# One block for the four phases, TensorE outside the joins, next phase's products, constants and rows early, and the directed phase's results two units later

## What is computed

```python
h = jnp.maximum(_layernorm(x, axis=-1), 0.0)
x = x + _L0_gnn_ref(h, adj, ...)   # attention, 12 heads, adj added to the scores, output projection Wo
x = x + _L1_gnn_ref(h, adj, ...)   # twice: scores h @ (h Wleft)^T and h @ (h Wright)^T under the graph, then relu(norm)
x = x + _L2_gnn_ref(h, adj, ...)   # twice: softmax(h h^T), then three linear maps for lower, own and upper neighbours
x = x + _L3_gnn_ref(h, adj, ...)   # attention, 12 heads, masked by adj, no output projection
...
hl = h @ wl.T + b_l
hs = h @ ws.T + b_s
hr = h @ wr.T + b_r
ctx = jnp.einsum('bij,bjd->bid', attn * upper, hl) + diag_a[..., None] * hs + jnp.einsum('bij,bjd->bid', attn * lower, hr)
o = (ctx - mean) / jnp.sqrt(var + LN_EPS) * g + beta
```

## Time and profile before

| | |
|---|---|
| median of 3 runs | 2728.71 us (2727.24 to 2729.51) |
| profiled execution | 2728.7 us |
| its span in the trace | 2727.0 us |
| mean granted clock of PE | 0.992 |
| PE busy | 2657.1 us (97%) |
| DVE, ACT, POOL busy | 1793.2, 1247.8, 1088.2 us (66, 46, 40%) |
| DMA | 183.87 MB, 67 GB/s over the span |

### The profile page before, as it was taken

How to read it: one execution, slowest core, us unless ns; L and a number is a source line. 1 busy time by engine, 2 the same in 40 slices (tenths; PEclk the granted TensorE clock), 3 DMA queues, 4 the chain that set the end, 5 groups by cost and what they waited for, 6 DMA issues and landing times. The chain is left out here.

```text
span 2727.0 us, 78262 instructions
## 1 busy us (share of the span) xinstructions
PE 2657.1 (97%) x31118; PEld 2315.9 (85%) x31118; DVE 1793.2 (66%) x4041; ACT 1247.8 (46%) x2184; POOL 1088.2 (40%) x1075
## 2 busy tenths in 40 slices
PE   6999999998999999999989999999999989999998
PEld 5888888887888888888878888888888878898897
DVE  6777777774555555555477777877877875666664
ACT  4444444454454444445443333433433435565564
POOL 2343434443322332332233435344434444455455
PEclk9999999999999999999999999999999999999999
DMA  4222222224112212211221111111111112222221
GB/s 143 75 68 62 59 67 73 73 73 146 37 54 82 82 36 59 82 36 55 74 76 51 57 45 52 56 40 56 58 40 51 61 53 74 88 86 82 89 85 62
DMA packets 187135, 183.87 MB, mean 67 GB/s; under 512 B 79616, under 2 KB 186880, under 8 KB 187008
## 3 DMA queue, kind: packets, MB, share of 16 engines
q1 hardware_dynamic: 187008, 181.99, 21.8%
HBM read 131.61 MB, written 50.33 MB: 67 GB/s over the span
## 5 line engine op out<-in xcount | busy, mean ns | idle before, releaser
L58 PE MATMUL banks<-w_hi,hT_hi 128*128 128x384 f32 x1152 | 402.0, 349 | 8.0 <-PEq L2517 7.0
L58 PE MATMUL banks<-hT_hi,w_hi 128*128 128x512 f32 (+1 forms) x954 | 367.7, 385 | 23.5 <-DVE l_qT L582 13.0
L58 PE MATMUL banks<-w_hi,hT_lo 128*128 128x384 f32 x1152 | 387.9, 337 | 0.0
L58 PE MATMUL banks<-w_lo,hT_hi 128*128 128x384 f32 x1152 | 387.4, 336 | 0.0
L58 PE MATMUL banks<-hT_hi,w_lo 128*128 128x512 f32 (+1 forms) x954 | 356.6, 374 | 0.0
L58 PE MATMUL banks<-hT_lo,w_hi 128*128 128x512 f32 (+1 forms) x954 | 355.6, 373 | 0.0
L1294 ACT ACTIVATE l_m<-banks 128x512 f32<-128x512 f32 x192 | 114.8, 598 | 397.5 <-PE banks L58 393.6
L305 POOL TENSOR_TENSOR l_s_d<-l_s_b,l_mx 128x768 f32<-128x768 f32 x128 | 188.7, 1474 | 222.4 <-DVE l_mx L607 207.2
L58 PE MATMUL banks<-w_hi,l_hT_hi 128*128 128x384 f32 x768 | 267.6, 348 | 5.1 <-DVE l_left L2137 3.5
L58 PE MATMUL banks<-w_hi,l_hT_lo 128*128 128x384 f32 x768 | 257.6, 335 | 0.0
L58 PE MATMUL banks<-w_lo,l_hT_hi 128*128 128x384 f32 x768 | 257.1, 335 | 0.0
(11 more groups left out here) (208 smaller groups left out, 6131.8 us busy)
## 6 DMA issues: line engine op xcount, KB each, us to landing
after_l<-l_xr SPq DMA_DIRECT2D x192, 192.0 KB, 1.9
l_xl<-after_l SPq DMA_DIRECT2D x37, 768.0 KB, 4.7
l_xr<-after_l SPq DMA_DIRECT2D x32, 768.0 KB, 4.5
xa<-in_x SPq DMA_DIRECT2D x16, 768.0 KB, 5.4
l_xr<-in_x SPq DMA_DIRECT2D x64, 192.0 KB, 2.4
l_xr<-after_l SPq DMA_DIRECT2D x64, 192.0 KB, 2.4
out_x<-l_xr SPq DMA_DIRECT2D x64, 192.0 KB, 1.9
xa<-after_l SPq DMA_DIRECT2D x11, 768.0 KB, 7.0
```

The source lines that it names most:

```text
L58: last = nc.tensor.matmul(out, lhs[a](c), rhs[b](c), start=(m == 0), stop=(m == n - 1))
```

## The change

All phases share one block, so that the barriers are gone. Each of DVE, ACT and POOL adds 1 to a new semaphore `ended` when its part of a phase is over; DVE, ACT, POOL and SP wait for all three before they touch the next phase (a multiple of 3), since tiles of one phase lie where those of the last lay. PE does not wait for it: it goes on into the next phase behind waits for single results (`shared["l2_ended"]` and the like hold a semaphore and its last count).

The first products of the next phase get banks of their own: four instead of two at the end of l0, two of them earlier in the last turn; six (left, right and own product of two tiles) at the end of l1; six queries and keys and two values at the end of l2. Constants, `adj` and, where their buffer is free, rows of the next phase are loaded in the phase before. The `handed_over` memsets move from DVE to POOL, before the last turn. The last results of l0, l1 and l3 are made on DVE (`own_result`, `centred`, `scaled`) where POOL made them or two engines passed them to and fro. The opening loads the first rows in two halves and each of Wq and Wk on its own semaphore, takes statistics a pair of tiles at a time, and makes products as soon as a weight is split. In the directed phase the results of a layer-1 unit (`finishes`) are added to `x` in the next layer-1 unit, two units later, and not in the layer-0 unit between; the first turn is written out ahead of the loop.

```diff
-    block = ctx.enter_context(nc.Block())
...
-            sp.dma_start(xl[:], rows(x_in, 0)).then_inc(xl_in, 16)
-            load_weights(sp, raw, own_weights, shared["w_loaded"])
-        n_consts = 0
-        for dst, src in biases(bv, out_bias, b_q, b_k, beta):
-            sp.dma_start(dst, src).then_inc(consts, 16)
...
+            first = rows(x_in, 0)
+            sp.dma_start(xl[:, 0:2, :], first[:, 0:2, :]).then_inc(xl_first, 16)
+            sp.dma_start(xl[:, 2:TILES, :], first[:, 2:TILES, :]).then_inc(xl_in, 16)
+            for s, signal in enumerate((wq_in, wk_in, shared["w_loaded"], shared["w_loaded"])):
+                sp.dma_start(raw[:, s], own_weights[s].rearrange("(c p) n -> p c n", p=P)).then_inc(signal, 16)
...
+            sp.wait_ge(shared["ended"], 3 * 3)
+            sp.wait_ge(stored, stored_before)
...
+            hT_parts(0, 0)
+            hT_parts(0, 1)
+            weights((0,))
+            hT_parts(0, 2)
+            hT_parts(0, 3)
+            weights((1,))
             statistics(1)
             shifts(1)
...
+        def product_of_next(j):
+
+            s, c = j // KC, j % KC
+            pe.wait_ge(w_lo_set, n_w + s + 1)
+            weight = tuple((lambda k, w=w: w[:, slot_of(s), k, c * P:(c + 1) * P]) for w in (w_hi, w_lo))
+            split_matmul(nc, banks[:, (1, 0, 2, 3)[j], :], weight, h_cols(slice(0, COLS))).then_inc(shared["m_done"], 1)
...
+            else:
+                pe.wait_ge(y_read, i * TILES - 1)
+                product_of_next(0)
...
             else:
-                pe.wait_ge(w_lo_set, n_w + 1)
                 pe.wait_ge(y_read, i * TILES)
-                product_of_next(0)
+                product_of_next(1)
             pe.wait_ge(eT_set, i * TILES + 3)
             exp_transposes(i, 3)
             if ahead:
                 pe.wait_ge(v_set, n * TILES + 1)
                 keys(n, 0)
             else:
-                product_of_next(1)
+                pe.wait_ge(eT_set, i * TILES + TILES)
+                out_transposes(i, 0)
             wait_apart(o_set, i * 2 + 1)
...
+                product_of_next(2)
+                product_of_next(3)
...
+            ended = shared["l2_ended"]
+            h_all = h_cols(slice(0, COLS))
+
+            def first_product(bank, s, c, signal):
+                split_matmul(nc, banks[:, bank, :], w_cols(s, slice(c * P, (c + 1) * P)), h_all).then_inc(signal, 1)
+
+            def first_values(t):
+                split_matmul(nc, banks[:, 6 + t, 0:D], h_cols(slice(t * P, (t + 1) * P)), w_cols(V, slice(0, D)))\
+                    .then_inc(v_done, 1)
+
+            pe.wait_ge(*ended["hT_set"])
+            pe.wait_ge(*ended["left_set"])
+            pe.wait_ge(*ended["w_lo_set"])
+            first_product(0, Q, 0, q_done)
+            pe.wait_ge(*ended["right_read"])
+            first_product(1, K, 0, k_done)
+            pe.wait_ge(*ended["s_set"])
+            first_product(2, Q, 1, q_done)
+            pe.wait_ge(*ended["self_set"])
+            first_product(3, K, 1, k_done)
+            first_product(4, Q, 2, q_done)
+            pe.wait_ge(*ended["hT_hi_set"])
+            first_product(5, K, 2, k_done)
+            pe.wait_ge(*ended["c_set"])
+            first_values(0)
+            first_values(1)
             pe.wait_ge(zeroed, 2)
-            wait_apart(k_set, 3)
+            pe.wait_ge(q_set, KC)
+            pe.wait_ge(v_set, 2)
+            wait_apart(k_set, KC)
             scores(0, 0)
             scores(0, 1)
-            values(0, 1)
             turns(pe, plain_turn)
 
...
+        sp.wait_ge(stored[1], stored_before[1])
+        load_rows(0, 1)
+        for k, name in enumerate(("L2_gnn_bl", "L2_gnn_br", "L2_gnn_bs")):
+            sp.dma_start(shared["l2_biases"][:, k], a[name][0].partition_broadcast(P)).then_inc(shared["l2_b_in"], 16)
...
+        centred(0)
+        centred(1)
+        last_scale(0)
+        centred(2)
...
+        step.catch_up(step.n - 3)
+        own_result(0)
+        step.catch_up(step.n - 2)
+        own_result(1)
+        step.catch_up(step.n - 1)
+        own_result(2)
+        step.catch_up(step.n)
+        own_result(3)
+        nc.vector.memset(shared["ends"][:, 2:3], 0.0).then_inc(shared["ended"], 1)
...
+            before = Unit(u.n - 2, u.q - 1, 1, 0) if finishes(u) else below if is_last(u) else None
...
-            left_copy(u, 1)
-            if ends:
-                result(below, 0)
-                result(below, 1)
+                left_copy(u, 1)
...
-            self_copy(u, 0)
+            if before is not None:
+                result(before, 0)
+                result(before, 1)
+            if below is not None:
...
             passed(0)
-            self_copy(u, 1)
-            if ends:
-                result(below, 2)
-                result(below, 3)
+            if below is not None:
+                self_copy(u, 1)
+            if before is not None:
+                result(before, 2)
+                result(before, 3)
...
+        dve.wait_ge(shared["ended"], 2 * 3)
+        dve.wait_ge(*shared["l1_ended"]["stored"])
...
+                right_part(u, 2)
+                passed(above, 1)
+                wait_apart(self_set, 2)
+                delta_transposes(u)
+                left_part(u, 3)
+                context(u, 0)
+            else:
                 left_part(u, 0)
...
+        ended, first = shared["l1_ended"], Unit(0, 0, 0, 0)
+
+        def first_product(bank, t, s, signal):
+            split_matmul(nc, banks[:, bank, 0:D], h_cols(first, t), projection(first, s)).then_inc(signal, 1)
+
+        pe.wait_ge(*ended["hT_set"])
+        pe.wait_ge(*ended["u_read"])
+        products(first)
+        pe.wait_ge(*ended["w_lo_set"])
+        pe.wait_ge(*ended["lin_set"])
+        first_product(0, 0, LEFT, left_done)
+        first_product(1, 0, RIGHT, right_done)
+        first_product(3, 1, LEFT, left_done)
+        pe.wait_ge(*ended["rows_set"])
+        first_product(4, 1, RIGHT, right_done)
+        pe.wait_ge(*ended["h_set"])
+        transposes(KC, rows_of[0], 0)
+        first_product(6, 0, SELF, self_done)
+        first_product(7, 1, SELF, self_done)
         schedule(unit, loop)
...
+        block = shared["block"] = ctx.enter_context(nc.Block())
```

More of the change, by code:

```diff
@@ L344, in projected_turn @@
             residual(i, 3)
-            result(i, 0)
-            if not ahead:
-                for t in (1, 2, 3):
-                    result(i, t)
+            if ahead:
+                result(i, 0)
         def plain_turn(i, opening, ahead, further):
@@ L1233, in ending @@
             root(i, k, 1)
-            if k >= 2:
-                for x in range(PAIR if isinstance(i, int) and i == last and k == 3 else TILES):
+            if k >= 2 and not (isinstance(i, int) and i == last and k == 3):
+                for x in range(TILES):
                     affine(i, k, x)
@@ L1317, in unit @@
             m_part(i, k, 1)
-            if not tail:
-                weight(CARRIED)
             ended(0)
@@ L1322, in unit @@
             m_part(i, k, 2)
-            if not tail:
-                weight(CARRIED + 1)
             ended(2)
@@ L1327, in unit @@
             m_part(i, k, 3)
+            if not tail:
+                weight(CARRIED)
             m_part(i, k, 4)
+            if not tail:
+                weight(CARRIED + 1)
             m_part(i, k, 5)
@@ L1354, in _ @@
         turn(last, False)
-        for x in range(TILES):
-            norm_rows(last, 3, x)
+        nc.scalar.activation(shared["ends"][:, 1:2], ident[:, 0:1], ACT.Copy).then_inc(shared["ended"], 1)
     @block.vector
@@ L1493, in unit @@
             passed(1)
+            if not tail:
+                dve.wait_ge(consts, 80)
+                dve.wait_ge(zeroed, 8)
             lin_copy(i, k, 0)
@@ L1792, in directed_phase, with finishes @@
     last = turns - 1
-    block = ctx.enter_context(nc.Block())
+    block = shared["block"]
     def pair_of_units(j):
         return Unit(2 * j + 2, j, 1, 0), Unit(2 * j + 3, j + 2, 0, 1)
+    def finishes(u):
+        return u.layer == 1 and not is_last(u) and not (isinstance(u.q, int) and u.q == 0)
     def is_last(u):
@@ L2030, in unit @@
                 next_weight(1)
+            if below is None:
+                weights((CARRIED, CARRIED + 1))
             passed(1)
@@ L2047, in loop @@
         def loop(turn):
-            with act.Fori(0, last) as j:
+            with act.Fori(1, last) as j:
                 turn(j)
         schedule(unit, loop)
+        nc.scalar.activation(shared["ends"][:, 1:2], ident[:, 0:1], ACT.Copy).then_inc(shared["ended"], 1)
     @block.vector
@@ L2199, in unit @@
         def unit(u, below, above, stats):
-            ends = below is not None and below.layer == 1
             carries = is_last(above)
+            before = Unit(u.n - 2, u.q - 1, 1, 0) if finishes(u) else below if is_last(u) else None
             def passed(c):
```

514 lines of the change are left out of this document (298 added, 216 removed).

## The result

The changed kernel takes 2692.95 us (median of 4 executions, 2689.87 to 2695.12) against 2728.4 of the kernel before, a ratio of 0.9868 with a 95% interval of 0.9856 to 0.988: 35 us faster. That is 16 us short of the 51.7 forecast, and 2.95 us above the range. The profiled execution was the fastest of the four, 2689.9 us with a span of 2688.1; it lies 38.8 us under the profiled one of before. Run again beside later experiments, the same kernel gave 2690.79 (2690.14 to 2692.88), ratio 0.9868, 0.9853 to 0.9884.

The account below looks back on a forecast made before the run. PE, busy 97%, was taken as the bound, leaving its idle, half-clock and stretched time to win. Terms 6.4 + 6.9 + 12.3 + 12.6 + 13.2 + 0.9 = 52.3 off 2728.7 gave 2676.4, forecast 2677; range 2667 to 2690.

Parts of the forecast that it names:

- Opening: Start of the kernel: separate weight semaphores, earlier loads and statistics, and later normalise shorten PE's waits; 6.4 us won.
- Join l0 to l1: End of l0: two more products cover 5.25 us idle and half-clock time returns; 6.9 us, bounds 3 and 7.
- Join l1 to l2: End of l1: six products replace the barrier stall and the slow stretch goes; 12.3 us, bounds 5 and 12.6.
- Rival B: At the joins PE stops for DVE or ACT, so they give half; +12 us, 2689, chance 0.15.
- Directed phase: l2's loop: 0.91 us won in each of 14 layer-0 units; 12.6 us, bounds 0 and 12.6.
- C: Directed loop gains nothing, its left copy being late for statistics and contexts too; +12.6 us, 2689, chance 0.12.
- E: Slower: four results in the layer-1 unit push its left copies late; 2741 at 4.6 us excess, chance 0.03.
- Join l2 to l3: End of l2: eight products cover 13.02 us idle and the half-clock loss returns; 13.2 us, bounds 8 and 15.7.
- rival F: No change: `ended` holds the engines as the barrier did and PE soon waits for them; 2728, chance 0.04.
- Tail: End of the kernel: POOL's last two additions of 1.94 us become DVE's at 0.52 each; 0.9 us won.
- The memsets: Before each join: ten POOL instructions ahead of the last turn, lying beside POOL's idle 60%; costed at nothing.
- Rival D: Code fetch shows on PE at each of three joins; 2683 at 2 us each, 2690 at 4.5, chance 0.04.

Follow-up runs that it names:

- its three causes mended: Changed kernel with tiles at the old kernel's places, carried-weight splits at the first directed unit's end, l2 constants loaded behind the next rows: 2678.51 us, ratio 0.9823.

## Why the forecast was wrong, step by step

- *Opening*, 6.4: measured 6.3, and the first product 5.0 earlier for 4.5. The second wait (1.88) went. That the sum agrees to 0.1 is luck, as the lead there differs by 4 us between traces with this opening. No run takes the parts of the opening one by one; they rest on the rows.
- *Join l0 to l1*, 6.9: 4.5. The mechanism was right, the products cover the end. The term was too large by PE's wait ahead of the last output's transposes, now 3.10 us and 1.89 before, and by the rows of l1's second group, which come late behind the constants of l2. For the results I had asked what their later stores and loads run into ("each has 50 us, nothing is near"), and not for these seven loads: the loads moved ahead have no term in the sum, though they stand in front of a load that DVE waits for. Moving them back took the gap away.
- *Join l1 to l2*, 12.3: 6.0, and this is the step that failed: "I leave 0.3 for a remaining wait". The bounds, 5 to 12.6, held it. A remaining wait of 4.56 us (1.04 and 3.52) stands there, and a stretch at half clock behind it that costs another 1.7: together the 6.3 us that are missing. The change moves `weights((CARRIED, CARRIED + 1))` to between `left_copy(u, 2)` and `left_copy(u, 3)`; I counted PE's six products and did not follow DVE's order in the first unit. With the splits behind the copies the join won 10.9. Rival B came true in size at this join alone, by another mechanism than `ended`.
- *Directed phase*, 12.6: 13.6 (14 times the 0.91 of the forecast is 12.7, not 12.6). Undoing the part alone took all of the loop's gain back. Rivals C and E are out.
- *Join l2 to l3*, 13.2: 14.1, with 0.36 us before the exponential's transposes. Holding PE showed 11 of it to be PE's going on; rival F is out. Of the other 3 us, the early loads and DVE's order were not taken apart.
- *Tail*, 0.9: −1.0. DVE's two additions take 1.03 us as forecast, but a stretch at half clock now lies over the last weighing but one (2.63 us for 1.60, below) and the transposes behind it, and costs some 1.7. It is not the change's: of the twelve traces with this tail four have this stretch and won −1.0 to −2.0 us, the eight others 0.3 to 1.8, 0.9 in the mean.

```profile
2712.60 1.60 PE L813 MATMUL banks<-l_vX,l_eT 64*64 64x33 f32 x96 [1.21 <-ACT l_eT L423]
```

```profile
2672.94 2.63 PE L890 MATMUL banks<-l_vX,l_eT 64*64 64x33 f32 x96 [1.21 <-ACT l_eT L459]
```

```profile
2684.76 1.03 DVE L711 TENSOR_TENSOR xr<-l_o_rows,xr 128x384 f32<-128x384 f32 x2
```

- *What the sum lacked*: 4.5 us in the l1 loop from where tiles lie, shown by the shifted kernel before (it lost 4.0) and by the three kernels with the old places (they lost nothing). The change moves buffers and tiny tiles in front of l1's; I looked for the cost of loads and instructions alone. The forecast sum with what each place differed by: 52.3 − 0.1 (opening) − 0.1 (l0) − 2.4 − 4.5 − 6.3 + 1.0 (directed loop) + 0.9 (last join) − 1.9 (tail) = 38.9, and the profile has 38.8.
- *The memsets*, put at nothing: they cost nothing that the trace shows, but not for the reason given. They don't stand before the last turn of the phase before; POOL runs them (nine or eight) behind the wait for `ended`, at 624.00, 1398.0 and 2217.0, and no engine waited for them.

Rival D needs a gap that the sequencer ends at a phase's first product. There is none: PE's idle time in the third join's window is 2.64 us, and it is made up of 1.59 and 0.69 before scores and 0.36 before transposes, all behind the first eight products. The row with 1.59 names no releaser, but PE's code waits there for the value copies, and ACT ended the last of them at 2225.64, 0.2 us before PE went on:

```profile
2224.30 1.34 ACT L454 ACTIVATE l_vX<-banks 64x192 f32<-64x192 f32 x4 [0.22 <-PE banks L58]
```

The page "Runtime: NRT & Kernel Launch" of the Trainium skill, section "Instruction fetch mechanics", says that a taken branch out of the window of two pages stalls. The branch at L824 shows no stall here; whether its target lay outside that window no run shows.

Two of the signs of being wrong came true beside the range: a slow stretch was left at the first and the second join, and each join kept more idle time than the 2 us named (5.1, 4.7 and 2.6).

With its three causes mended the change gives 2678.5 us, near the 2677 forecast; the mechanisms of the sum were there, and the forecast missed what the change did beside them. That the two numbers are so close is in part luck, as the sum's terms for the opening and the tail move by some us between executions.

## What to carry to other kernels

Line up two traces by the k-th matmul of the same kind and look at the lead from place to place: it finds losses that busy shares hide, such as a loop at 233 ns a matmul instead of 228. When a change adds tiles, buffers or small ones, look where the large ones come to lie, and keep it as it was until it is measured. And where a change lets one engine run ahead, read the other engines' new order up to the first thing it will wait for: splits of weights, or loads for the phase after next, cost what they stand in front of.

## What the runs showed of the hardware

- TensorE's pace depends on where in SBUF what it reads lies. Matmuls of 512 columns on l1's second h start 228 ns apart with that tile at byte 142976 or 149120, and on average 233 with it at 143008, 148704 or 148736 (the last is a multiple of 256); in the same loop those on the first h, whose tile did not move, kept their pace to 0.5 ns. In l2, with moving weights and a stationary h, it was 173 ns at 145216 and 175 at 145248. All tiles of a phase moved together, so which distance between which tiles decides was not found out. The Trainium skill's page "SBUF — State Buffer", section "Who interferes with whom", says that only the port pair shared by VectorE and GpSimd brings contention and that TensorE never waits on anyone; the kernel before and its shifted copy differ in no engine's work, so if the rule holds the loss is TensorE's own.
- Whether and when the clock falls behind the same stall differs between executions. The same kernel's opening was at 0.50 from 41.5 in one and from 44.0 in another, and the lead after it differed by 1.4 us. Behind the same wait of 3.52 us at the second join the clock fell in the changed kernel (0.51 above), and it stayed up in the kernel with `ends` padded, where that join won 7.6 us and not 6.0:

```profile
1416.20:1419.70 3.50, 3.50 (x63) 2.31 (x64) 2.54 (x4) 0.83 (x1) 0.00 (x0) 1.00 0.00 0
```

  Such stretches, and one wait for rows that was 0.58 us in one execution and 3.08 in another, are as large as what single edits win. PE stands less in the changed kernel (38.2 us of the span outside its busy time, 2688.1 − 2649.9, for 69.9 before), but a narrower spread is not shown: four executions of it spread over 5.3 us and later four over 2.7, those of the kernel before over 2.3 (four) to 6.4 us (nine).
